# A four-layer graph network in fp32: VectorE takes one operand from PSUM, the output jobs are laid out anew, and layer 2's product with the coefficient runs as four activations of ScalarE

## The reference, cut to what matters

```python
# layer 0: relu(x @ Ws.T + bs + agg @ Wn.T + bn), agg = segment_sum(w * x[src], dst), w from the edge features
# layer 1: K = 10 steps with w = rsqrt(deg_row[row] * deg_col[col])
out = h = x
for _ in range(10): out = segment_sum(out[col] * w[:, None], row) * 0.9 + h * 0.1
out = out / theta
# layer 2: K = 16 steps with self loops
h = x
for _ in range(16): h = 0.9 * segment_sum(norm * h[row], col) + 0.1 * x
# layer 3: h = prelu(gcn_conv(x, W1, b1)); h = prelu(gcn_conv(h, W2, b2))
```

## Time and profile before

| | us |
|---|---|
| median of 3 runs | 9375.67 (9374.41 to 9386.8) |
| profiled execution, its own time | 9382.56 |
| its span, first to last instruction | 9380.8 |
| busy in the span: PE, PEld, DVE, ACT, POOL | 5571.1, 4454.3, 4873.3, 1985.4, 6899.3 |
| costliest group: gathers of line 1830, `l_g<-tab,l` (layer 2), x2940 | 2844.8 busy, mean 968 ns |
| the same in layer 1, `l_g<-tab,XM`, x1764 | 1772.5 busy, mean 1005 ns |
| scans of line 2014, x1248 | 1592.0 busy, mean 1276 ns |

### The profile page before, as it was taken

How to read it: one execution, slowest core, us unless ns; L and a number is a source line. 1 busy time by engine, 2 the same in 40 slices (tenths; PEclk the granted TensorE clock), 3 DMA queues, 4 the chain that set the end, 5 groups by cost and what they waited for, 6 DMA issues and landing times. The chain is left out here.

```text
span 9380.8 us, 85944 instructions
## 1 busy us (share of the span) xinstructions
PE 5571.1 (59%) x23638; PEld 4454.3 (47%) x23638; DVE 4873.3 (52%) x12137; ACT 1985.4 (21%) x5391; POOL 6899.3 (74%) x7074
## 2 busy tenths in 40 slices
...
GB/s 145 132 182 101 94 98 105 100 99 99 109 99 101 100 99 89 112 68 75 94 110 109 113 113 107 109 107 109 96 95 94 98 95 93 96 96 87 89 46 38
DMA packets 896288, 938.67 MB, mean 100 GB/s; under 512 B 370431, under 2 KB 786305, under 8 KB 895711
## 3 DMA queue, kind: packets, MB, share of 16 engines
...
## 5 line engine op out<-in xcount | busy, mean ns | idle before, releaser
L1830 POOL DMA_INDIRECT l_g<-tab,l x2940 | 2844.8, 968 | 933.5 <-issue 877.5
L2014 DVE TENSOR_TENSOR_SCAN l_w<-l_m,l_w,bank 96x512 f32<-96x512 bf16 x1248 | 1592.0, 1276 | 2965.2 <-PE bank L1857 2962.9
L1857 PE MATMUL bank<-ident,l_g 128*96 128x128 f32 x5096 | 1211.5, 384 | 1967.6 <-DMA l_g<-tab,l 964.8
L1830 POOL DMA_INDIRECT l_g<-tab,XM x1764 | 1772.5, 1005 | 602.3 <-issue 523.7
L1857 PEld LDWEIGHTS bank<-ident,l_g 128*96 128x96 f32 x5096 | 807.0, 177 | 2427.0 <-DMA l_g<-tab,l 1090.1
L1874 PEld LDWEIGHTS bank<-ident,l_w 96*128 96x128 f32 x6272 | 1606.4, 328 | 353.4 <-issue 290.4
L1874 PE MATMUL bank<-ident,l_w 96*128 96x96 f32 x6272 | 1512.3, 405 | 9.4 <-DVE l_w L2014 9.2
L1865 PE MATMUL bank<-XM,ident 128*128 128x384 f32 x1568 | 959.1, 707 | 0.0
L373 ACT ACTIVATE tail_sc<-tail_mv,eps_x 125x4 f32<-125x4 f32 (+1 forms) x149 | 44.3, 297 | 2294.6 <-DVE tail_mean L365 2294.6
L393 ACT ACTIVATE tail_y<-bank,tail_of,tail_sc 125x96 f32<-125x96 f32 (+1 forms) x596 | 208.7, 431 | 1300.4 <-DVE tail_of L384 1300.4
L285 PE MATMUL bank<-tail_xt,v 96*96 96x500 f32 (+1 forms) x298 | 279.0, 1038 | 323.2 <-ACT tail_xt L280 323.2
...
## 6 DMA issues: line engine op xcount, KB each, us to landing
...
l_g<-tab,l POOLq DMA_INDIRECT x2940
l_g<-tab,XM POOLq DMA_INDIRECT x1764
...
```

Of the source, the lines that this page charges most:

```text
L1830: nc.gpsimd.indirect_dma_start(out=tile(G[q % RG], t), out_offset=None, in_=tables[0:table_at + (2 - p % 2) * TR, :] if p else first, in_o ...
L1857: last = nc.tensor.transpose(a_bank(q)[0:D, u:GE:U], G[q % RG][:, u * D:(u + 1) * D], self.ident[:, :])
L2014: v.tensor_tensor_scan(out=W[q % RW][:, :], data0=masks[q % RM][:, :], data1=a_bank(q)[0:D, :], initial=W[(q - 1) % RW][:, GE - 1:GE] if q ...
```

## The change

It does these things:

- Layer 1: `pass_on` writes `O` as before, `update` follows it at once and adds the bank itself (unmultiplied) to `T`; the factor comes once, in pass 8, out of `lcoef` (`icoef` is gone). The bank is free again after `update` and no longer after `pass_on`. In the last pass the product is written to the bank.
- Layer 2: `sum_up` writes its sum to the bank, and ScalarE makes the product with `coef_d` out of the bank into `T`, as four activations (one for each 96 columns), ahead of its job steps and behind `prepare` in the same step. TensorE's `add_own` waits for that product of three groups before.
- Jobs: the second activation of each `rectify` writes back into its bank, `merge_first` reads that bank, and `merge_second` writes its first result there; buffers `down` are gone. `rectify_first` comes at offset 4, `merge_first` at 5.
- Begin of the jobs: node jobs every 6 slots in pass 0 (6 jobs), every 4 in passes 1 to 7 (10 each), every 8 in pass 8 (5), and 19 in 80 new slots that lie beside the gathering of layer 2's own rows (VectorE takes about 1.8 of them before each of its first 44 groups there); slot jobs begin in pass 0 of layer 2 at slot 0 and end in pass 7.
- Lots: passes 1 to 10 of layer 2 send 2 groups, passes 11 to 15 send 3; before, it was 2 and 3 in turn from pass 2 on.

```diff
@@ -44,8 +44,9 @@
 LAG = 12
 HALF, FIRST = 25, 2
 RECORDS_AT, SUMS_AHEAD, ENDS = NGP, 3, 5
-NODE_PERIOD, SLOT_PERIOD = 4, 6
 SLOTS = 40
+NODE_PERIODS = (6,) + (4,) * 7 + (8,)
+OWN_SLOTS, OWN_PERIOD, SLOT_PERIOD = 80, 4, 6
 OWN = 25
 AHEAD_GROUPS = 2
 BOTH_FIRST = 39
@@ -53,9 +54,9 @@
 PACE = 2
 SR = 3
 LOT_ROOM = (4, 3)
-LOTS = (2, 3) * 7 + (4, 3, 4, 3)
-LOT_SENT = {"smooth": tuple((p, 0) for p in range(2, 16)) + ((15, 49),) * 2, "conv1": ((0, 49),) * 2}
-LOT_LOADED = {"smooth": tuple((p, 42) for p in range(1, 15)) + ((15, 12), (15, 24)), "conv1": ((0, 8), (0, 20))}
+LOTS = (2,) * 10 + (3,) * 5 + (3, 4, 3, 4)
+LOT_SENT = {"smooth": tuple((p, 0) for p in range(1, 16)) + ((15, 49),) * 2, "conv1": ((0, 49),) * 2}
+LOT_LOADED = {"smooth": tuple((p, 42) for p in range(15)) + ((15, 12), (15, 24)), "conv1": ((0, 8), (0, 20))}
 EPS = 1e-5
 GD = U * D
 NP_ = 125
@@ -119,9 +120,13 @@
         nodes, slots = [("nodes", n) for n in range(NJ // U)], [("slots", n) for n in range(NGP)]
         self.jobs = nodes + slots
         self.count = len(self.jobs)
-        first_slot = (len(nodes) - 1) * NODE_PERIOD + SLOT_PERIOD
-        self.begin = [n * NODE_PERIOD for n in range(len(nodes))] + [first_slot + n * SLOT_PERIOD for n in range(NGP)]
+        layer1 = (K1 - 1) * SLOTS
+        begin = [p * SLOTS + n for p, period in enumerate(NODE_PERIODS) for n in range(0, SLOTS - period + 1, period)]
+        begin += [layer1 + n * OWN_PERIOD for n in range(len(nodes) - len(begin))]
+        self.begin = begin + [layer1 + OWN_SLOTS + n * SLOT_PERIOD for n in range(NGP)]
         self.at_slot = {slot: n for n, slot in enumerate(self.begin)}
+        turned = sorted({slot + offset - layer1 for slot in self.begin for offset in (2, 4, 7, 10)})
+        self.own_steps = [slot for slot in turned if 0 <= slot < OWN_SLOTS]
...
-        self.up, self.down = ([tmp(n, [D, GE]), spare[0:D, k * GE:(k + 1) * GE]] for k, n in enumerate(("up", "down")))
+        self.up = [tmp("up", [D, GE]), spare[0:D, 0:GE]]
...
-        n = due(5)
+        n = due(4)
...
-        n = due(6)
+        n = due(5)
...
-            pe.wait_ge(self.rect1, n)
+            pe.wait_ge(self.merged1, n)
...
         a.activation(self.up[self.copy(n)][:, 0:w], z, ACT.Relu, bias=self.p.c1[:, 0:1])
-        a.activation(self.down[self.copy(n)][:, 0:w], z, ACT.Relu, bias=self.p.c1n[:, 0:1], scale=-1.0).then_inc(self.rect1, 1)
+        a.activation(z, z, ACT.Relu, bias=self.p.c1n[:, 0:1], scale=-1.0).then_inc(self.rect1, 1)
 
     def merge_first(self, dve, n):
         w = U * self.parts(n)
         dve.wait_ge(self.rect1, n + 1)
-        self.nc.vector.scalar_tensor_tensor(out=self.up[self.copy(n)][:, 0:w], in0=self.down[self.copy(n)][:, 0:w], scalar=self.p.neg[:, 0:1],
-                                            in1=self.up[self.copy(n)][:, 0:w], op0=ALU.mult, op1=ALU.add).then_inc(self.merged1, 1)
+        up, z = self.up[self.copy(n)][:, 0:w], self.p.bank[5][0:D, 0:w]
+        self.nc.vector.scalar_tensor_tensor(out=up, in0=z, scalar=self.p.neg[:, 0:1], in1=up, op0=ALU.mult, op1=ALU.add
+                                            ).then_inc(self.merged1, 1)
...
-            pe.wait_ge(self.rect2, n)
+            pe.wait_ge(self.merged2, n)
...
-        a.activation(self.down[self.copy(n)][:, 0:w], z, ACT.Relu, bias=self.p.c2n[:, 0:1], scale=-1.0).then_inc(self.rect2, 1)
+        a.activation(z, z, ACT.Relu, bias=self.p.c2n[:, 0:1], scale=-1.0).then_inc(self.rect2, 1)
 
     def merge_second(self, dve, n):
         w = U * self.parts(n)
         dve.wait_ge(self.rect2, n + 1)
-        up, v = self.up[self.copy(n)][:, 0:w], self.nc.vector
-        self.link(dve, v.scalar_tensor_tensor(out=up, in0=self.down[self.copy(n)][:, 0:w], scalar=self.p.neg[:, 0:1], in1=up,
-                                              op0=ALU.mult, op1=ALU.add))
-        v.tensor_tensor(out=up, in0=up, in1=self.xt[n % 2][:, 0:w], op=ALU.add).then_inc(self.merged2, 1)
+        up, z, v = self.up[self.copy(n)][:, 0:w], self.p.bank[6][0:D, 0:w], self.nc.vector
+        self.link(dve, v.scalar_tensor_tensor(out=z, in0=z, scalar=self.p.neg[:, 0:1], in1=up, op0=ALU.mult, op1=ALU.add))
+        v.tensor_tensor(out=up, in0=z, in1=self.xt[n % 2][:, 0:w], op=ALU.add).then_inc(self.merged2, 1)
...
-                    tails.turn(kind, eng, (p + (K1 - 1) * smooth) * SLOTS + g - 1)
+                    return tails.turn(kind, eng, p * SLOTS + g - 1 + ((K1 - 1) * SLOTS + OWN_SLOTS) * smooth)
+
+            def between(kind, eng, slot):
+
+                return tails.turn(kind, eng, (K1 - 1) * SLOTS + slot)
...
-                        pe.wait_ge(summed.sem, summed.at + q - RB + 1)
+                        if q - RB < updates:
+                            pe.wait_ge(made.sem, made.at + q - RB + 1)
+                        else:
+                            pe.wait_ge(summed.sem, summed.at + q - RB + 1)
...
-                            pe.wait_ge(made.sem, made.at + q - RB + 1)
+                            pe.wait_ge(ready.sem, ready.at + q - RB + 1)
...
+                if smooth:
+                    for slot in range(OWN_SLOTS):
+                        last = between("pe", pe, slot)
+                        if slot in self.tails.own_steps:
+                            last.then_inc(stepped.sem, 1)
...
+                def pass_on(p, g):
+
+                    q = p * NGP + g
+                    act.wait_ge(summed.sem, summed.at + q + 1)
+                    for t in range(g * U, (g + 1) * U):
+                        last = a.activation(tile(group(T, g), t), tile(b_bank(q), t), ACT.Copy, scale=self.coef_d[:, t:t + 1])
+                    last.then_inc(made.sem, 1)
...
@@ -1976,11 +2016,17 @@
                                             scale=s1[g % SR][:, u:u + 1])
                     last.then_inc(normed.sem, 1)
 
+                if smooth:
+                    for slot in range(OWN_SLOTS):
+                        between("act", act, slot)
                 for p in range(K):
                     for g in range(NGP + (1 if looped and p < final else 7 + late)):
                         if p == 0 and before is not None and g < NGP:
                             prepare(g)
                         if p < final:
+                            for n in backs(g):
+                                if smooth:
+                                    pass_on(p, n)
                             if g < NGP:
                                 background("act", act, p, g)
                             continue
...
@@ -2036,49 +2085,42 @@
                     if p == final:
                         link(v.scalar_tensor_tensor(out=there, in0=group(XS, g), scalar=10.0, in1=there, op0=ALU.mult,
                                                     op1=ALU.add))
-                    v.tensor_tensor(out=there, in0=b, in1=there, op=ALU.add).then_inc(summed.sem, 1)
+                    v.tensor_tensor(out=there if p == final else b, in0=b, in1=there, op=ALU.add).then_inc(summed.sem, 1)
 
                 def pass_on(p, g):
 
                     q = p * NGP + g
                     at = slice(g * U, (g + 1) * U)
-                    if power:
-                        o = O[q % RO][:, :].rearrange("p (u d) -> p u d", d=D)
-                        if back_at(g) == NGP:
-                            step_back(dve, q)
-                        free(dve, q)
-                        if q >= RO:
-                            dve.wait_ge(ready.sem, ready.at + q - RO + 1)
-                        of, by = b_bank(q)[:, 0:GD].rearrange("p (u d) -> p u d", d=D), self.lcoef if p == final else self.coef_s
-                    else:
-                        dve.wait_ge(summed.sem, summed.at + q + 1)
-                        o = of = group(T, g).rearrange("p (u d) -> p u d", d=D)
-                        by = self.coef_d
-                    v.tensor_tensor(out=o, in0=of, in1=by[:, at].unsqueeze(2).to_broadcast([P, U, D]), op=ALU.mult
-                                    ).then_inc(made.sem, 1)
+                    b = b_bank(q)[:, 0:GD]
+                    if back_at(g) == NGP:
+                        step_back(dve, q)
+                    free(dve, q)
+                    o, by = b if p == final else O[q % RO][:, :], self.lcoef if p == final else self.coef_s
+                    v.tensor_tensor(out=by_row(o), in0=by_row(b), in1=by[:, at].unsqueeze(2).to_broadcast([P, U, D]),
+                                    op=ALU.mult).then_inc(made.sem, 1)
 
                 def update(p, g):
 
                     q = p * NGP + g
-                    there, o = group(T, g), O[q % RO][:, :]
-                    dve.wait_ge(made.sem, made.at + q + 1)
+                    there, b = group(T, g), b_bank(q)[:, 0:GD]
                     if p == 0:
-                        v.tensor_copy(there, o).then_inc(ready.sem, 1)
-                    else:
-                        dve.wait_ge(ready.sem, ready.at + q - NGP + 1)
-                        if p != final - 1:
```

(46 more changed lines are left out.)

48 lines of the change are left out of this document (31 added, 17 removed).

## The result

The changed kernel takes 9127.94 us (median of 4 runs, 9125.88 to 9136.57), the kernel before beside it 9375.04 (9363.08 to 9386.8): a ratio of 0.9738, with an interval of 0.9721 to 0.9755. The profiled execution took 9125.88 us with a span of 9124.1, against 9382.56 and 9380.8 before, so the two traces differ by 256.7 us where the medians differ by 247. The granted clock is the same (0.634, before 0.635). The forecast median was 9161 with 9125 to 9210 as its own range: the result is 33 us under the forecast and only 3 us above the lower end.

The account below looks back on a forecast made before the run. GpSimd was taken to set the pace in nearly all passes. Terms -99 - 64 - 12 - 36 - 14 + 12 - 4 + 2 = -215 us took 9375.7 to 9161 us (own range 9125 to 9210; 8 in 10, 9120 to 9245).

Parts of the forecast that it names:

- What bounds the kernel: GpSimd sets the pace in nearly all passes; any gain must shorten an indirect DMA or remove a GpSimd stall.
- the held gathers: Busy time of gathers above 0.944 us each: -99 us forecast in layer 1, -64 us in layer 2.
- Two SBUF inputs: VectorE operations with two SBUF inputs lengthen GpSimd's indirect DMAs; removing them gives -99 us in layer 1, -64 in layer 2.
- Rival 2: Lengthening comes from VectorE's activity, not the inputs' place alone: 9243 us if half stays, 9324 if all; chance 0.07.
- Stalls in layer 1: GpSimd waits less in layer 1: -12 us in pass 0, -36 in pass 8, -14 idle after pass 8.
- Pass 0 of layer 2: ScalarE's product closes a loop through prepare, transposes, scan and sum; 6.2 us a slot, 310 us for 297.9, so +12.
- Boundaries: The 14 later pass ends of layer 2: nine with 8 sends at 11.9 us, five with 12 at 15.8; -4 us.
- Own rows: 19 node jobs beside the gathering of layer 2's own rows cost +2 us for more weighs (0 to +25).
- Rival 3: Jobs beside layer 2's own rows hold up VectorE or ScalarE: +56 us, 9217 us; chance 0.10.
- Rivals 1: Rival 1: ScalarE's product holds up all of layer 2, 0.85 us a slot over 290 slots: 9408 us; chance 0.04.
- Rival 4: First pass of layer 2 is cheap, with the clock high throughout and a product of 1.1 us: 9136 us; chance 0.07.
- Rival 5: The change does little: held time moves to weigh, stalls stay, all bad ends: 9291 us; chance 0.02.

Follow-up runs that it names:

- the new operands alone: Changed kernel's operands and ScalarE's product, with begin of jobs and lots as in the kernel before (offsets stay new): 9167.58 us, ratio 0.9786.
- the new order alone: Kernel before with the changed kernel's begin of jobs, offsets and lots; all VectorE inputs old, layer 2's product on VectorE: 9241.37 us, ratio 0.9858.

## Why the prediction was right, and where its terms were off

**What bounds the kernel** held. GpSimd set the pace in nearly every pass; the gain is 173 us of shorter DMAs and 84 us of stalls, and VectorE's 402 us show up nowhere, ScalarE's 736 only in pass 0 of layer 2. That the result is inside the forecast's own range owes something to luck: the terms that missed, pass 0 (22 us), the boundaries (10) and the held gathers (8), missed almost all to the same side, and 3 us more would have left it.

**Two SBUF inputs** held as cause and as size. Layer 1 gave -103 for -99, layer 2 -68 for -64. That it is the inputs' place was argued from two timeline pairs and is now shown: by 56 us for the sum moved to SBUF, by 686 further operations that lengthened nothing, and by 961 ns as the longest gather once no such operation was left. The 0.12 us that I took for a `weigh` at a random phase was too much. By the form above it is 0.073, and 130 operations (81 `weigh`, 49 of pass 8) make 9.5 us where layer 1 shows 1860.5 - 1850.2 = 10.3. That the two sums agree is in part chance: only 5.8 us of it are in gathers that start inside such an operation. Nor does an operation hold a gather for at most its own length, as the prediction had it: in layer 1 of the kernel before, a gather that started 0.04 us into an `update` of 0.54 us took 0.72 us longer (1.66 us at 1674.86). Rival 2 has fallen.

**Stalls in layer 1** held: -14, -37 and -16 us for -12, -36 and -14. The reason that I gave for pass 8, five jobs for ten, isn't the only one: the kernel with the new operands alone kept ten jobs and had no such stall either. The new order, with fewer jobs in the pass, is what brought the idle time after it from 23 to 12 us.

**Pass 0 of layer 2** is the step that failed: the closed loop was right (three edits that open it or take the product out give 255 to 257 us), the size wrong by 22 us, and the sign with it. The timeline of its loop, a slot without a job's step on ScalarE (start us, length us, instruction, [idle before]):

```profile
4300.35 1.28 DVE L2063 TENSOR_TENSOR_SCAN l_w<-l_m,l_w,bank 96x512 f32<-96x512 bf16 x1 [3.86 <-PE bank L1881]
...
4301.55 0.53 DVE L2088 TENSOR_TENSOR bank<-bank,T 128x384 f32<-128x384 f32 x1
4302.12 1.03 ACT L1979 ACTIVATE T<-bank,coef_d 128x96 f32<-128x96 f32 x4 [2.50 <-DVE bank L2088]
...
4303.02 1.17 ACT L1961 ACTIVATE l_g<-l_g,dinv_e 128x96 f32<-128x96 f32 x4
...
4304.25 1.07 PE L1881 MATMUL bank<-ident,l_g 128*96 128x128 f32 x4 [1.14 <-ACT l_g L1961]
...
4305.35 1.28 DVE L2063 TENSOR_TENSOR_SCAN l_w<-l_m,l_w,bank 96x512 f32<-96x512 bf16 x1 [3.27 <-PE bank L1881]
```

Every link is there in the order predicted: scan, sum, product, `prepare`, transposes, scan. Such a slot takes 4305.35 - 4300.35 = 5.0 us where I had 5.2, and the product holds up ScalarE for 4303.02 - 4302.12 = 0.90 where I took 1.2. The row shows why a duration is the wrong measure: four activations last 1.03 us together and one 0.34, but the next instruction starts 0.90 after the first, since one begins before the one ahead has ended. A product costs the loop its spacing (0.23 us for 96 columns), not its duration. Over 48 slots 0.3 us make 14 us; in the slot above the other links take 0.1 more than I had (`prepare` to transposes 1.23 for 1.15), which would give 5 of them back. The six slots of one job take 5.1, 6.2, 5.6, 5.9, 5.0 and 6.3 us, and all 40 slots with jobs a mean of 5.74, for the forecast 6.2: 18 of the 22 us. Here the job's steps count by their spacing too, as a pair of rectifies holds ScalarE up for 1.14 us and not 1.34. The sum also had 49 steps from the first scan to the last, where 49 scans have 48 between them.

The Trainium skill had the better figure. VectorE: DVE Perf Modes, section "The TRN2 errata", gives 0.223 us for an activation of 96 columns from PSUM, and so an estimate of 0.89 us for four; the trace has 0.90 in the loop. I had weighed it and preferred the duration of a row with bias and scale. Of that page's table, the 62 cycles that a PSUM input costs VectorE are still not in the traces: the same product took 557 ns from the bank and 561 from SBUF.

**Boundaries.** I forecast -4 and they gave -14. I had read 10.9 us of the earlier trace rows as the drain. They are the eight sends themselves, which last 8.2 us there, and nine gaps of 0.30. In the changed kernel the sends last 7.8, which makes 10.6 with the gaps, and what the drain adds behind them is 0 to 2 us; ScalarE's products make no difference (average of 8-send boundaries 11.2 with them, 11.2 without). The 11.9 for a boundary with 8 sends was 0.7 too high, nine times, which is 6 of the 10 us; another 3 are in the boundaries of before, which add up to 192.7 and not to 190.

**Own rows**: +5 for +2, inside the bounds. VectorE's splitting still reads two SBUF inputs, and so does `weigh`. Without the jobs beside them (the new operands alone) the own rows are busy for 189.9 us, with them for 193.6; with the jobs in their old operands (the new order alone) it is 202.4. Rival 3 has fallen, and the first gather of pass 0 wasn't late for it.

**Rivals 1, 4 and 5.** In passes 1 to 14 of layer 2 nothing waits for ScalarE's product: putting it on VectorE in pass 0 alone gave all that putting it there everywhere gave. Rival 4 had a number near the result (9136) and half the right reason: a cheap product, but a clock of 0.68 in this pass and not full. The boundaries and the held gathers brought the rest of the way, which that rival had not. Rival 5 didn't happen.
